# Two graph-transformer layers on one core: where the last head pair's logits are issued, and which PSUM banks attention starts in

## The reference, cut to what matters

```
q, k, v = (x @ qkv_w.T) split in 3, 8 heads of 64
qw = splat_weights(q);  kw = splat_weights(k)        # 16 numbers per token and head
logits = einsum('bihs,bjhs->bijh', qw, kw) / temp
attn = softmax(logits, axis=2)
out = einsum('bijh,bjhd->bihd', attn, v)
return out @ out_w.T
```

## Time and profile before

| | |
|---|---|
| median of 3 runs | 861.49 us (861.15 to 863.32) |
| the profiled execution, its time | 859.79 us |
| the profiled execution, its span (first to last instruction) | 858.0 us |
| mean granted TensorE clock, share of full speed | 0.960 |
| PE busy | 775.5 us, 90% of the span |
| DVE busy | 616.8 us, 72% |
| ACT busy | 381.5 us, 44% |

### The profile page before, as it was taken

One profiled execution on the slowest core, in us unless ns is written; L12 is line 12 of the kernel. 1 busy time (PEld: TensorE's weight loads), 2 busy tenths in 40 slices (PEclk: granted clock), 3 DMA queues, 4 the chain that ended last, 5 costly groups with the idle time before them and its releaser, 6 DMA issues. The chain is left out here.

```text
span 858.0 us, 11649 instructions
## 1 busy us (share of the span) xinstructions
PE 775.5 (90%) x4058; PEld 572.3 (67%) x4058; DVE 616.8 (72%) x1225; ACT 381.5 (44%) x583; POOL 117.2 (14%) x91
## 2 busy tenths in 40 slices
PE   4989999999999982699599999899989999999998
PEld 3777887888778861465287777665556566665876
DVE  7777887776758757698864424288986888898646
ACT  2342343343214412375321202855632888887453
POOL 3000000000000005010454000444340013000000
PEclk9999999999999995699589999999999999999999
DMA  5563322310302142999320301100000000010002
GB/s 183 155 204 114 100 74 58 89 41 8 123 0 99 50 176 98 264 377 317 108 99 1 99 0 50 50 0 2 1 2 3 3 1 1 1 56 2 1 1 98
DMA packets 48152, 66.63 MB, mean 78 GB/s; under 512 B 4268, under 2 KB 22460, under 8 KB 48095
## 3 DMA queue, kind: packets, MB, share of 16 engines
q1 hardware_dynamic: 43903, 56.22, 20.3%
q0 software_dynamic: 2384, 6.92, 2.5%
q10 hardware_dynamic: 1808, 2.75, 0.9%
HBM read 56.38 MB, written 9.50 MB: 77 GB/s over the span
## 5 line engine op out<-in xcount | busy, mean ns | idle before, releaser
L974 PE MATMUL bank<-xT,slot 128*128 128x512 f32 (+1 forms) x248 | 107.2, 432 | 2.7 <-DVE xT L1782 2.3
L975 PE MATMUL bank<-xT,slot 128*128 128x512 f32 (+1 forms) x248 | 99.0, 399 | 0.0
L976 PE MATMUL bank<-xT,slot 128*128 128x512 f32 (+1 forms) x248 | 98.5, 397 | 0.0
L1485 ACT ACTIVATE slot<-bank 128x512 fp32r<-128x512 f32 (+3 forms) x60 | 34.2, 586 | 137.7 <-PE bank L1241 56.3
L974 PE MATMUL bank<-slot 128*128 128x512 f32 (+1 forms) x212 | 83.2, 392 | 5.2 <-DVE slot L1782 1.9
L974 PE MATMUL bank<-slot,xT 128*128 128x512 f32 (+1 forms) x192 | 78.7, 410 | 2.8 <-DVE slot L2296 1.9
L976 PE MATMUL bank<-slot 128*128 128x512 f32 (+1 forms) x212 | 80.8, 381 | 0.0
L975 PE MATMUL bank<-slot 128*128 128x512 f32 (+1 forms) x212 | 80.8, 381 | 0.0
L2321 DVE TENSOR_REDUCE key<-bank 128x2 f32<-128x1024 f32 x64 | 74.3, 1218 | 6.9 <-PE bank L1301 6.9
L976 PE MATMUL bank<-slot,xT 128*128 128x512 f32 (+1 forms) x192 | 76.1, 396 | 0.0
L975 PE MATMUL bank<-slot,xT 128*128 128x512 f32 (+1 forms) x192 | 75.9, 395 | 0.0
(11 more groups left out here) (339 smaller groups left out, 1637.3 us busy)
## 6 DMA issues: line engine op xcount, KB each, us to landing
arena<-in_ewT SPq DMA_DIRECT2D x16, 1024.0 KB, 11.1
arena<-in_edge_attr SPq DMA_DIRECT2D x16, 512.0 KB, 3.9
wraw<-in_qkvT SPq DMA_DIRECT2D x3, 1024.0 KB, 5.1
expert_rows<-rows SPq DMA_DIRECT2D x1, 2560.0 KB, 13.8
wraw<-in_L_ffn_expert_b POOLq DMA_DIRECT2D x16, 160.0 KB, 5.9
expert_results<-wraw ACTq DMA_DIRECT2D x16, 160.0 KB, 5.7
xn<-in_x SPq DMA_DIRECT2D x4, 512.0 KB, 6.9
wraw<-in_L_mix_w_qkv SPq DMA_DIRECT2D x2, 1024.0 KB, 8.1
```

The costliest lines, as they stand in the source:

```text
L974: pe.matmul(out, L[1], R[0], start=start, stop=False, **kw)
L975: pe.matmul(out, L[0], R[0], start=False, stop=False, **kw)
L976: return pe.matmul(out, L[0], R[1], start=False, stop=stop, **kw)
L1485: act.activation(h, src, kw.pop("func", ACT.Copy), **kw).then_inc(hi_done, 1)
```

## The change

Three places change. The logits of the last pair get a new layout: two steps behind the first value product and two in the middle of each of the other seven (before: 2 behind the first, 2 inside and 2 behind the second and third, 2 inside the fourth, fifth and sixth, none with the last two). The attention units exchange their banks: even units go to banks 4 and 5, odd units to banks 2 and 3. And the explicit wait for the low half of ("V1", 5) in bank 5 moves from unit 1 to unit 0, which now writes that bank.

```diff
@@ plan_jobs
         elif step[0] == "E":
-            add(*step, bank=2 + 2 * (step[1] % 2))
+            add(*step, bank=4 - 2 * (step[1] % 2))
@@ logits_about
     if job[0] == "V1":
-        return ((0, 2), (2, 2), (2, 2), (2, 0), (2, 0), (2, 0), (0, 0), (0, 0))[job[1]]
+        return (0, 2) if job[1] == 0 else (2, 0)
@@ TensorE, attention
                 if step[0] in ("E", "oU", "oT"):
                     open_bank(*step)
-                if step == ("E", 1):
+                if step == ("E", 0):
                     emptied(pe, "V1", 5)
```

## The result

| | before | changed |
|---|---|---|
| median of 20 runs | 862.23 us (859.16 to 866.14) | 858.85 us (855.84 to 862.54) |
| ratio, 95% interval | | 0.9960 (0.9949 to 0.9972) |
| the profiled execution: its time, its span | 859.79, 858.0 us | 860.58, 858.8 us |
| its granted clock | 0.960 | 0.958 |
| PE busy | 775.5 us | 776.9 us |

The changed kernel is 3.4 us (0.40%) faster; 859.0 was predicted, with 2.5 us of gain. Yet its profiled execution is 0.8 us longer than the one of before. One execution each therefore shows nothing of the gain as a whole; the stage has to be read by itself. Beside later experiments one execution of the kernel before took 1579.98 us and one of the changed kernel 2648.07 us, both with a granted clock of 1.00; all ratios and means leave them out.

The account below looks back on a forecast made before the run. Early value products were taken to wait for DVE's reduces, and attention to be bound by TensorE. Two waits of 1.25 us removed, all other terms 0, gave 861.49 - 2.50 = 858.99, so 859.0 us; range 857.9 to 861.2.

Parts of the forecast that it names:

- Where the time was: Value products: TensorE's second logit pair, issued 2.3 us after the first, waits for DVE's reduces, 1.25 us each time.
- The layout, -2.50: Value products: moving logit pairs from behind V1 and V2 into V6 and V7 removes two waits of 1.25 us.
- mT 2 beside the reduces: In V6, DVE's 0.58 us for transpose mT 2 fits beside the reduces with 0.14 to spare; cost 0, bounds 0 and 0.6.
- The exchange of banks: Start of attention: banks 4 and 5 spare unit 0 a wait for the last reduce, worth up to 0.74 us less what ACT hides.
- Unit 1's wait: Start of attention: unit 1 starts 0.33 us late behind the last reduce, hidden by 0.07; cost 0, bounds 0 and 0.33.
- DVE at the end of the stage: V7's low half on DVE ends at 660.71, before attention's first cast is due at 660.87: hidden, 0.16 us to spare.
- Attention passes it on: Attention: TensorE sets the pace, not a fixed time, so all of the 2.50 us gain reaches the end.
- Rival C: Each product from V2 to V7 waits as V1 does: stage 5.0 us longer, 866.5 us; chance 0.04.
- Rival D: The gain is taken back in attention because something there is due at a fixed time: 861.5 us; chance 0.09.
- Rival A: The hand-over to attention eats a part, delaying the first exponentials: gain 1.5 to 2.2 us, 859.3 to 860.0; chance 0.17.
- rival B: More than counted: V1's wait also shortens or restarts cost less; gain 3.1 us, time 858.4; chance 0.10.
- The rule on the clock: Waits from 632 to 649 us would cost clock by the skill page; the trace showed granted clock 1.00, so nothing was added.

Follow-up runs that it names:

- all_inside: Changed kernel with two logit steps inside every value product, first included, and last key weights made ahead of the reduces: 859.56 us, 0.9966 of the kernel before.
- all_behind: Changed kernel with two logit steps behind every value product, the last included, none inside: 861.31 us, 0.9989 of the kernel before.
- before_again: The kernel before, unedited, run and profiled once more: 862.84 us, ratio 1.0005.
- after_again: The changed kernel, unedited, run and profiled once more: 858.83 us, 0.9947 of the kernel before.
- layout_only: Changed kernel with the new logit layout but attention's old banks (even units in 2 and 3): 860.25 us, 0.9972 of the kernel before.
- four_waits: Changed kernel with logit steps 2 behind V0, 2 inside and 2 behind V1 to V3, 2 inside V4, none later: 862.27 us, 1.0002 of the kernel before.
- low_early: Changed kernel with the second low quarter of the value weights made with the first, ahead of the reduces: 856.08 and 856.43 us, 0.9928 and 0.9930 of before.

## Why the prediction was right

- **Where the time was.** Three waits of 1.25 us, set by two pairs of logits 2.3 us apart. Shown: one, two, three and four such places give 27.6, 28.84, 30.1 and 31.39 us. A layout without any (all_inside, all_behind) gives 25.4 to 25.5, which is 27.6 less one wait of 1.25 and less the 0.905 of the pair that stands outside V0 to V7 there.
- **The layout, -2.50.** Read as -2.57 in the profile (30.17 to 27.60), and 2.46 between before_again and after_again. The rest of V1 kept its wait, as was said.
- **mT 2 beside the reduces, 0 (bounds 0 and 0.6).** 0: V6 has its 3.63 us; the cover was 0.11, not 0.14.
- **The exchange of banks.** It was said to be worth up to 0.74 less what ACT hides. layout_only shows 0.91, more than that bound: unit 0 is 0.79 late and its second matmul 0.90, the slow restart included, and ACT hid none of it. This term was mis-sized, but it does not stand in the sum, as the banks were exchanged.
- **Unit 1's wait, 0 (bounds 0 and 0.33).** 0.33 late and hidden, as worked out, by a margin of about 0.1 (its second matmul is listed to 663.58 + 0.40, its exponential was due at 663.16 + 0.92). all_behind shows what comes when the margin is gone: the same wait, 2.35 us long, and unit 0 0.87 us later took back the 2.2 us that its layout had won over the changed kernel's.
- **DVE at the end of the stage, 0 with 0.16 to spare.** This step failed: V7's low half was 0.35 later than worked out, and the first cast of attention 0.10 late. It cost nothing, since DVE was idle for 0.40 us ahead of the second cast, and the first product with the values still came 4.04 us behind the first exponential. The cover was luck here, not the one that was worked out.
- **Attention passes it on.** 195.6 us from the first exponential to the end before and after.
- **Rival C** (every product waits) fell: no wait from V2 on. **Rival D** fell too. **Rival A** did not come about.
- **The number itself, 859.0 against 858.85.** That they agree to 0.15 us is luck. The forecast started from 861.49 us, the median of three runs, where 20 runs gave 862.23: 0.7 too low. It took off 2.5 us where 3.4 were measured: 0.9 too little. The two nearly cancel.
- **What the sum left out** is about 1 us. The medians lie 3.4 to 4.0 us apart and not 2.5, the ratios are 0.9960, 0.9947 and 0.9958 against a worked-out 0.9971. Two of the three intervals still hold that value; all three medians on the same side make chance unlikely, not excluded. It is not rival B, since neither V1's wait nor a restart changed. I had read the clock from one profile, in which no low stretch stood near the stage, and concluded that the clock has no part in this. In the other profile of the same kernel it stood in V0 and at the start of attention. The mean clocks of the runs would account for 0.8 to 1.2 us, which is the right size; the cause stays open.
- **The rule on the clock.** The prediction set aside, on a single trace, what the Trainium skill, page "TensorE: Matmul & The Clock Gate", section "A second HAM failure mode: psum-queue depth-cycling", says: that frequent short idle times between groups of matmuls, in a kernel that cycles through PSUM banks, move the clock up and down. For the waits that this change removes, that was right: in none of 13 profiles did a low stretch follow the waits of up to 0.63 us inside the value products. The low stretches near the stage stand behind the 1.9 us ahead of V0 and behind the waits at the start of attention, in some profiles and not in others, and the change leaves both places as they are.

The measured gain is clear of 0.3% only in its median; the interval reaches from 0.28 to 0.51%. The forecast of "within 0.3%" with 0.40 for "faster" rested on 2.5 us against a bound of 2.6, and the part that the sum left out decided it.

## What to carry to other kernels

When two engines share a stage, look at the spacing of what one hands to the other, not only at the busy shares: DVE had work for 3.0 us of each 3.6, and TensorE still lost 1.25 us wherever two portions came 2.3 us apart. Spread them evenly, and keep the last portion off the banks that the next stage needs first: without the second half of this change a third of the first was lost. Under 0.5%, judge an edit by the distances inside its stage in several profiles and by medians of many runs, since stretches of low clock of 1.4 us each come and go around it.

## What the runs showed of the hardware

- The same program has different stretches of the 1.2 GHz level in different executions. Near this stage they are two, in V0 and in the first units of attention, each worth 1.3 to 1.5 us (V0 4.37 to 4.60 us instead of 3.04 to 3.09; first exponential to the end 197.0 to 197.2 us instead of 195.5 to 195.7, all_behind with its longer waits aside). The one in V0 stands in 6 of the 11 profiles with 1.9 us of idle time ahead of V0, the one at the start of attention in 5 of all 13. A third place is at about 548 us, behind 2.14 us of idle time of TensorE that all 13 profiles have: there the first profile of the kernel before and that of all_inside have one (granted clock 0.61 from 548 to 550 us in the former), the other 11 have none.
- The mean clock differs from kernel to kernel by more than between sets of runs of one kernel (0.9606, 0.9614 and 0.9608 for the changed one, 0.9594, 0.9595 and 0.9595 for the one before): 0.9573 (all_behind, 12 runs), 0.9586 (all_inside, 10), 0.9595 (before, 82), 0.9608 (changed, 39), 0.9618 (four_waits, 12), 0.9620 and 0.9629 (low_early, 6 and 8). It does not follow the number of waits. That it follows where a layout puts the idle times in time is a guess; it was not tested. Removing the idle time ahead of V0 altogether is the one edit here after which that stretch never showed (two profiles).
- Two logit steps, 4 matmuls of 48 rows, cost 0.905 us between products, though they are not four matmuls at the ordinary rate. In the trace of the kernel before the two matmuls of a step start together, at 653.85 and at 654.18; the last matmul ahead of them starts at 653.53, the next two at 654.51 and 654.85. So there is a start every 0.32 to 0.34 us around the change between 48 and 128 rows, where the stream of 128-row matmuls has one every 0.23.
